# A four-layer network on one NeuronCore: VectorE's work, DRAM round trips and TensorE forms rearranged in layer 0 and layer 3

## The chip, the core and the metric

The kernel runs on one core of one Trainium2 chip. The metric is the device time of one execution in microseconds (us). The profile is one execution taken by the hardware profiler. PE is TensorE (its matmuls; an fp32 matmul is recorded as two passes), PEld its weight load, DVE is VectorE, ACT is ScalarE, POOL is GpSimd, SP is SyncE, whose queue issues most DMAs. Lines (L271) are lines of the kernel before.

## The reference, cut to what matters

The input x has the shape [2, 96, 48, 48]. Four layers follow one another, each of the form x + layer(groupnorm(x)). Layer 0 is a selective scan in four directions with E = 192 channels, N = 16 states and L = 2304 positions:

```python
xz = einsum('bchw,oc->bohw', x, in_proj_w)
xi, z = split(xz, 2, axis=1)
xi = silu(conv2d(xi, conv_w, conv_b, groups=E, pad=1))     # 3x3 depthwise
xs = stack([xf, xf[..., ::-1], xt, xt[..., ::-1]], axis=1)  # four directions
dlt, b, c = ...                                             # projections of xs
dlt = softplus(dt_proj(dlt) + dt_proj_b)
dA = dlt[..., None] * A_log
phi = exp(-cumsum(dA))
h = phi * cumsum(dlt * b * xs / (phi + 1e-12))
y = einsum('bkdln,bknl->bkdl', h, c) + Ds
ys = y1 + y2 + y3 + y4      # each turned back into image order
yn = layernorm over channels(ys) * ln_g + ln_b
u = yn * z                  # then 1x1, depthwise 3x3, 1x1, SE gate
```

Layer 1 forms sums of products of channel pairs, layer 2 is a 9x9 depthwise convolution. Layer 3 splits the channels in three: a gated 3x3 convolution (conv0), a fractional Fourier transform with a gated channel mix and its inverse, and a real FFT with the same; the three parts, concatenated, go through a 3x3 convolution with 96 channels (conv2), whose result is added to x. Both spectral mixes add a constant per channel: `Mix = group_conv(Mix, conv05_w * Y) + conv05_b`.

## The kernel before, in words

Every stage is a function with a block of its own: each engine has its instruction list, engines meet at semaphores, and at the end of a block all of them meet. The order within an engine is the order of the code. `ps` is all of PSUM, eight banks of 512 fp32 columns. The E x batch = 384 rows of layer 0 lie in T = 3 tiles of 128 partitions.

- **l0_project** (L182 to L284). TensorE makes xi and then z in chunks of 384 columns, 18 each; ScalarE copies them out of PSUM, xi into a padded image `pad`, z into `Z`. Each tile has nine depthwise taps of 2304 columns, 27 in all: ScalarE forms eight as products (L250), three of them as a tile's first term and five that GpSimd adds (L284), and VectorE does the other 19 as multiply-adds (L271). Then Silu (L254).
- **l0_steps** (L287 to L592). The step sizes softplus(x), made from e = exp(-|x|) and ln(1 + e) with a correction for the rounding of 1 + e, in 36 units of 768 columns. Per unit TensorE projects into a PSUM slot (L431; two slots for the first eight units, three afterwards), ScalarE does Abs, Ln of the unit before, Exp (L485, L490, L493), VectorE does four operations (`rounded` L521, L527, L532, and L537 that makes `dl` and frees the slot), GpSimd forms v = dl * xs (L585), and SP stores dl and v to DRAM. GpSimd and SP also do the weight products of layer 1 here, `wa*ma + wb*mb` in cuts of 8 (L565, L567, L570), with loads and stores between those of dl and v.
- **l0_scan** (L595 to L868). 36 units of 16 steps of 768 columns. In each step ScalarE forms decay and tanh, VectorE scans (L800) and multiplies (L774, L781), GpSimd multiplies (L811, L820), and TensorE broadcasts rows of b and c (L704) and sums the 16 products in PSUM with an identity (L737). After a unit ScalarE copies the sum out (L832) and its queue stores it to DRAM `y`, 36 stores of 384 KB.
- **l0_norm** (L871 to L1005). The twelve `y` arrays are loaded again and nine VectorE additions turn and add them (L971, L973), then the layernorm: mean by TensorE (L924), centring (L980), squares, variance (L930), reciprocal (L988), root, spread to the rows (L939), and the product with Z (L1004).
- **l3_gates** (L1510 to L1653). Gates on small matmuls; SP stores the normalised input, loads it turned (`xh`, L1551) and spreads three shifted copies of 32 channels into `G0` row by row (L1558).
- **l3_forward** (L1656 to L1827). Transform over rows (L1722 and L1728), over columns (L1736 for the fractional one, L1746 for the FFT, two products each, summed in PSUM), the channel mix in five chunks `fr` (L1756) with a one-row matmul that adds the constant (L1758), VectorE's phases as tables of 2304 columns (L1803, L1804), and a mix for the FFT (L1763). Results go to DRAM.
- **l3_inverse** (L1830 to L2024). conv0 for both images (L1935, 36 matmuls), four inverse transforms (L1944, L1952, L1959, L1968), results `P` and `F` stored to DRAM (L1904, L1909) and loaded back turned into `cat` (`to_cat`, L1898), all by SP, each store waited for before its load is issued; then conv2 (L1977) and the final addition into X (L2023). A last block stores X.

## Time and profile before

| | us |
|---|---|
| median of 3 runs | 3286.42 (3284.29 to 3290.19) |
| the profiled execution | 3293.45 |
| its span, first to last instruction | 3291.6 |
| l0_project | 25.7 to 113.9 |
| l0_steps | 114.4 to 346.9 |
| l0_scan | 350.9 to 2075.2 |
| l0_norm | 2078.0 to 2191.6 |
| l3_gates (after its group norm) | 3003.1 to 3021.3, next stage from 3032.4 |
| l3_forward | 3032.4 to 3126.5 |
| l3_inverse | 3130.8 to 3283.0 |
| output | to 3291.6 |

The start and end of a stage are the first and last record of its lines. Because engines meet at every stage's end, each stage can be read for itself: which engine's work ended it, and what that engine waited for. An engine that is busy for most of the span (VectorE 81%) is not the bound in every stage.

### The profile page before, as it was taken

How to read it: one execution, taken by the hardware profiler on the slowest of the kernel's cores; microseconds unless marked ns; L12 is line 12 of the kernel's file. 1: busy time of each engine (PE TensorE's matmuls, PEld its weight loads, DVE VectorE, ACT ScalarE, POOL GpSimd, SP SyncE). 2: the span in 40 equal slices, each digit the busy share in tenths (PEclk: the TensorE clock that was granted, in tenths of full speed). 3: DMA queues.
4: the chain of work that ended last, by engine and by line, in shares of the span. 5: the costliest groups of instructions: out<-in, count | busy, mean ns of one | idle time of the engine just before them, and what ended most of it. 6: DMA issues, size and time to landing. Idle time of an engine off the chain costs nothing. (4 is left out here: it accounts for less than half of the span.)

```text
span 3291.6 us, 24792 instructions
## 1 busy us (share of the span) xinstructions
PE 2159.3 (66%) x7226; PEld 1034.3 (31%) x7226; DVE 2659.7 (81%) x2092; ACT 1607.6 (49%) x2295; POOL 2126.9 (65%) x1113
## 2 busy tenths in 40 slices
PE   3454366666666666666666666488409897893958
PEld 1221123222332323323232333232105453452634
DVE  7677699999999999999999999668846566896200
ACT  4454477677767766777677677135300000641120
POOL 4166699999999999999999999107230000791000
PEclk8776699999999999999999999766759898896679
DMA  1176443344344333443444343500058885004050
GB/s 43 50 206 224 148 127 117 115 124 127 110 128 127 123 110 122 128 125 112 124 127 121 111 125 112 202 0 0 0 160 316 274 311 173 22 8 62 15 65 22
DMA packets 161258, 388.16 MB, mean 118 GB/s; under 512 B 60577, under 2 KB 70441, under 8 KB 147945
## 3 DMA queue, kind: packets, MB, share of 16 engines
q1 hardware_dynamic: 155400, 368.37, 36.8%
q10 hardware_dynamic: 5730, 18.29, 1.6%
q8 instruction: 56, 0.92, 0.1%
q14 instruction: 72, 0.59, 0.1%
...
## 5 line engine op out<-in xcount | busy, mean ns | idle before, releaser
L811 POOL TENSOR_TENSOR l0c_r<-l0c_r,l0c_v 128x768 f32<-128x768 f32 x576 | 1040.1, 1821 | 23.9 <-DVE l0c_r L774 22.8
L839 ACT ACTIVATE ps<-l0c_dlt,l0c_na 128x512 f32<-128x512 f32 (+1 forms) x1152 | 626.0, 575 | 517.0 <-DVE l0c_h L800 492.7
L820 POOL TENSOR_TENSOR l0c_hcp<-l0c_cb,l0c_h 128x768 f32<-128x768 f32 x384 | 698.7, 1820 | 0.7 <-DVE l0c_h L800 0.6
L800 DVE TENSOR_TENSOR_SCAN l0c_h<-ps,l0c_h,l0c_r 128x768 f32<-128x768 f32 x384 | 693.2, 1805 | 5.0 <-issue 5.0
L864 ACT ACTIVATE l0c_r<-l0c_S,l0c_floor,l0c_na 128x768 f32<-128x768 f32 x576 | 583.5, 1014 | 14.2 <-ACT l0c_y L832 14.2
L737 PE MATMUL ps<-l0c_hcp,net_ident 128*128 128x512 f32 (+1 forms) x1536 | 582.3, 502 | 9.0 <-ACT l0c_y L832 6.0
L704 PE MATMUL ps<-l0c_Bp,l0c_sel 96*128 96x512 bf16 (+1 forms) x1152 | 294.1, 338 | 439.9 <-DVE l0c_hcv L781 258.2
L774 DVE SCALAR_TENSOR_TENSOR l0c_r<-l0c_r,ps 128x768 f32<-128x768 f32 x576 | 533.1, 925 | 6.8 <-PE ps L704 4.1
L737 PEld LDWEIGHTS ps<-l0c_hcp,net_ident 128*128 128x128 f32 x1536 | 269.7, 196 | 256.1 <-issue 199.4
L1297 PE MATMUL ps<-l_prod,l_wa 128*96 128x384 f32 (+1 forms) x888 | 291.3, 492 | 86.9 <-DVE l_prod L1281 86.9
L800 DVE TENSOR_TENSOR_SCAN l0c_h<-ps,l0c_r 128x768 f32<-128x768 f32 x192 | 334.9, 1744 | 0.0
L1281 DVE TENSOR_TENSOR l_prod<-l_base,l_other 128x2304 f32<-128x2304 f32 (+1 forms) x74 | 189.3, 2558 | 138.7 <-PE ps L1297 88.2
L737 PE MATMUL ps<-l0c_hcv,net_ident 128*128 128x512 f32 (+1 forms) x768 | 289.8, 500 | 1.1
L704 PEld LDWEIGHTS ps<-l0c_Bp,l0c_sel 96*128 96x128 bf16 x1152 | 86.0, 98 | 618.7 <-DVE l0c_r L774 526.7
...
L1297 PEld LDWEIGHTS ps<-l_prod,l_wa 128*96 128x96 f32 (+1 forms) x888 | 146.3, 165 | 231.3 <-issue 143.7
L1187 POOL TENSOR_TENSOR l_Z<-l_Z,l0f_prod 128x2304 f32<-128x2304 f32 x13 | 85.1, 6557 | 184.7 <-ACT l0f_prod L1108 184.1
...
L704 PE MATMUL ps<-l0c_Cp,l0c_sel 96*128 96x256 bf16 (+1 forms) x384 | 96.4, 333 | 158.9 <-DVE l0c_r L774 157.6
L781 DVE TENSOR_TENSOR l0c_hcv<-ps,l0c_h 128x768 f32<-128x768 f32 x192 | 181.9, 947 | 0.0
L1493 PE MATMUL ps<-l_rows,l_diag 128*128 128x384 f32 x450 | 154.7, 506 | 33.6 <-ACT l_diag L1399 19.3
L737 PEld LDWEIGHTS ps<-l0c_hcv,net_ident 128*128 128x128 f32 x768 | 134.6, 195 | 124.8 <-issue 99.1
...
## 6 DMA issues: line engine op xcount, KB each, us to landing
l0c_cb<-cf SPq DMA_DIRECT2D x768, 192.0 KB, 3.4
l_other<-po SPq DMA_DIRECT2D x72, 1152.0 KB, 5.1
...
l0n_yk<-y SPq DMA_DIRECT2D x9, 1152.0 KB, 8.4
```

The lines of the kernel that those rows point to most:

```text
L704: mm = pe.matmul(ps[:, lo:hi], sel[:, t % 2, n * 128:(n + 1) * 128], rows[:, i, lo - at:hi - at], start=True, stop=True)
L737: mm = pe.matmul(ps[:, lo:hi], ident[:, :], hc[:, lo - PY:hi - PY], start=(n == 0), stop=(n == N - 1))
L774: dve.scalar_tensor_tensor(rj, rj, 1.0, b_all, ALU.add, ALU.mult).then_inc(s_ub, 1)
L781: dve.tensor_tensor(hcv[:, dve_steps(j) % NHV, :], c_all, h[:, j % N, :], ALU.mult).then_inc(s_hv, 1)
L800: dve.tensor_tensor_scan(h[:, n, :], da[j % 2], r[:, j % NR, :], init, ALU.mult, ALU.add).then_inc(s_scan, 1)
L811: pool.tensor_tensor(r[:, j % NR, :], r[:, j % NR, :], v[:, (j // N) % 2, :], ALU.mult).then_inc(s_w, 1)
L820: pool.tensor_tensor(hcp[:, p % NHP, :], cb[:, p % NCB, :], h[:, e % N, :], ALU.mult).then_inc(s_hp, 1)
L839: act.activation(da[e % 2][:, part], dlt[:, i, part], ACT.Exp, scale=na[:, i, n:n + 1]).then_inc(done, 1)
L864: act.activation(r[:, j % NR, :], S[:, i, :], ACT.Tanh, bias=floor[:, :], scale=na[:, i, N + n:N + n + 1]).then_inc(s_tanh, 1)
L1281: dve.tensor_tensor(prod[0:n, s, :], base[0:n, s, :], other[0:n, s, :], ALU.mult).then_inc(s_prod, 1)
L1297: mm = pe.matmul(ps[0:C, c * BANK:c * BANK + CH], wa[0:height[i], i, :], prod[0:height[i], i % 3, c * CH:(c + 1) * CH], start=(i == 0), st ...
L1493: mm = pe.matmul(ps[:, o:o + CH], diag[:, tl, i, :], rows[:, tl, dy + 8 * c:dy + 8 * c + 8, dx:dx + W], start=(i == 0), stop=(i == NPE - 1))
```

## The change

It touches layer 0 up to its norm and layer 3; layers 1 and 2 and the ffn are as they were.

- **load, l0_project**: the projection's weights are loaded with x. Only the edges of `pad` are zeroed. xi's 18 chunks are copied out by ScalarE and VectorE in turn. Taps 0 to 2 become matmuls with diagonal matrices (made by GpSimd) into PSUM banks 0 to 5, VectorE does the six others on halves of a tile (1152 columns, 36 in all), the first of them reading PSUM. z's chunks lie between, through banks 6 and 7. GpSimd's additions and ScalarE's products are gone.
- **l0_steps**: u = 1 + e is made by ScalarE (Identity with a bias), then Ln(u); VectorE's L521 is gone and its next operation forms (u - 1) - ln. Four buffers of dl and v instead of three. v is stored one unit later than dl. The layer-1 weight products are no longer here. Z is stored to DRAM at the start (3.5 MB).
- **l0_scan**: the sum of a unit stays in SBUF, in `Y`, which takes Z's place, in image order. For the second to fourth direction TensorE adds what Y holds to the unit's sum with identity matmuls in steps 4 to 7 (27 units of 36), and ScalarE writes the whole back, the last direction with the scale and the sum of Ds. ScalarE's tanh runs one step late for five steps after that.
- **l0_norm**: no y loads, no additions. Z is loaded again. The layer-1 weight products are made here by GpSimd, in cuts of 5, with their loads and stores.
- **l3_gates**: G0's three copies are spread as whole contiguous rows of 2304 elements and the wrong edge columns zeroed afterwards.
- **l3_forward**: row transforms write two groups of partitions (0 and 64), so that the two column products become one matmul with twice the contraction: 192 passes of L1736 become 96, 384 of L1746 become 192. The one-row matmuls are gone; their term is a table `u1` that VectorE forms once and adds.
- **l3_inverse**: conv0 of the second image comes after the inverse transforms. P and F are stored by ScalarE's queue, each on a semaphore of its own; SP only loads. X is stored in 12 parts as conv2's chunks end.

Cut to its core, the diff is:

```diff
+                if j >= 2:
+                    pe.wait_ge(s_tap, OWN * (j - 2) + 1)
+                for i in range(MM):
+                    dy, dx = divmod(i, 3)
+                    for c in range(HB):
+                        y0 = 8 * (HB * half + c) + dy
+                        mm = pe.matmul(ps[:, bank(HB * (j % 2) + c)], diag[:, t, i, :],
+                                       pad[:, t, y0:y0 + 8, dx:dx + W], start=(i == 0), stop=(i == MM - 1))
+                mm.then_inc(s_sum, 1)
...
+                for n, i in enumerate(range(MM, TAPS)):
                     dy, dx = divmod(i, 3)
                     if n:
-                        dve.wait_ge(s_tap, sum(own[:t]) + n)
-                    dve.scalar_tensor_tensor(dst, pad[:, t, dy:dy + H, dx:dx + W], cw[:, t, i:i + 1], dst,
-                                             ALU.mult, ALU.add).then_inc(s_tap, 1)
+                        dve.wait_ge(s_tap, OWN * j + n)
+                    dve.scalar_tensor_tensor(
+                        dst, pad[:, t, r0 + dy:r0 + dy + 8 * HB, dx:dx + W].rearrange("p (c h) w -> p c h w", h=8),
+                        cw[:, t, i:i + 1], dst if n else total, ALU.mult, ALU.add).then_inc(s_tap, 1)
...
                     act.wait_ge(s_e, i)
-                    if i >= 2:
-                        act.wait_ge(s_a, i - 1)
-                    act.activation(ps[:, LN:LN + SEG], e[:, (i - 1) % NE, :], ACT.Ln, bias=1.0).then_inc(s_ln, 1)
+                    if i > NW:
+                        act.wait_ge(s_q, i - NW)
+                    act.activation(u[:, (i - 1) % NW, :], e[:, (i - 1) % NE, :], ACT.Identity, bias=one_col[:, :]
+                                   ).then_inc(s_u, 1)
                 if i < U:
                     act.wait_ge(s_ab, i + 1)
                     act.activation(e[:, i % NE, :], e[:, i % NE, :], ACT.Exp, scale=-1.0).then_inc(s_e, 1)
+                if i:
+                    act.wait_ge(s_u, i)
+                    if i >= 2:
+                        act.wait_ge(s_a, i - 1)
+                    act.activation(ps[:, LN:LN + SEG], u[:, (i - 1) % NW, :], ACT.Ln).then_inc(s_ln, 1)
...
-            def rounded(i):
-                dve.wait_ge(s_e, i + 1)
-                dve.tensor_scalar(wm[:, i % NW, :], e[:, i % NE, :], 1.0, -1.0, ALU.add, ALU.add).then_inc(s_wm, 1)
-
-            rounded(0)
             for i in range(U):
                 dve.wait_ge(s_ln, i + 1)
-                dve.wait_ge(s_wm, i + 1)
-                dve.tensor_tensor(ln, wm[:, i % NW, :], ln, ALU.subtract).then_inc(s_q, 1)
-                if i + 1 < U:
-                    rounded(i + 1)
+                dve.scalar_tensor_tensor(ln, u[:, i % NW, :], 1.0, ln, ALU.subtract, ALU.subtract).then_inc(s_q, 1)
...
+        def so_far(u):
+
+            t, k, c0 = place(u)
+            return scan_order(Y[:, t, :], k)[:, c0 // W:(c0 + SEG) // W, :]
+
+        def y_pieces(u):
+
+            k, full = place(u)[1], BANK // W
+            if k < 2:
+                flat = Y[:, place(u)[0], ::-1] if k else Y[:, place(u)[0], :]
+                c0 = place(u)[2]
+                return [(PY, PY + BANK, flat[:, c0:c0 + BANK]), (PY + BANK, PY + SEG, flat[:, c0 + BANK:c0 + SEG])]
+            rows, cut = so_far(u), BANK % W
+            return [(PY, PY + full * W, rows[:, 0:full, :]),
+                    (PY + full * W, PY + BANK, rows[:, full, 0:cut]),
+                    (PY + BANK, PY + BANK + W - cut, rows[:, full, cut:W]),
+                    (PY + BANK + W - cut, PY + SEG, rows[:, full + 1:SEG // W, :])]
...
+                if place(u)[1] and 4 <= n < 4 + len(y_pieces(u)):
+                    lo, hi, src = y_pieces(u)[n - 4]
+                    pe.matmul(ps[:, lo:hi], ident[:, :], src, start=False, stop=False)
...
+                src = y_all.rearrange("p (r c) -> p r c", c=W)
+                if k < K - 1:
+                    act.activation(so_far(u), src, ACT.Copy).then_inc(s_evac, 1)
+                else:
+                    act.wait_ge(s_dsum, 1)
+                    act.activation(so_far(u), src, ACT.Identity, scale=0.5, bias=dsum[:, t:t + 1]).then_inc(s_evac, 1)
...
+                late = 0 < u < U and LAG + 3 <= n < LAG + 8
+                if j < J and not late:
+                    if 0 < u and n == LAG + 8:
+                        tanh(j - 1)
+                    tanh(j)
+                elif late and n > LAG + 3:
+                    tanh(j - 1)
...
+                lo, hi = max(0, 1 - i), L - max(0, i - 1)
                 for b in range(B):
-                    sp.dma_start(G0[C3 * i:C3 * i + C3, b, 1:1 + H, lo + 1 - i:hi + 1 - i],
-                                 by_image(XG[0:C3, b, :])[:, :, lo:hi]).then_inc(s_spread, 16)
+                    sp.dma_start(G0[C3 * i:C3 * i + C3, b, :, :].rearrange("c h w -> c (h w)")[:, W + lo:W + hi],
+                                 XG[0:C3, b, lo + i - 1:hi + i - 1]).then_inc(s_spread, 16)
...
-                        for s in range(2):
-                            mm = pe.matmul(ps[BC * q:BC * q + BC, o:o + UH],
-                                           A2[:, :, :, s, u].rearrange("p b c -> p (b c)"),
-                                           fw[:, s, UH * q:UH * q + UH], start=(s == 0), stop=(s == 1))
+                        mm = pe.matmul(ps[BC * q:BC * q + BC, o:o + UH], A2[:, :, :, u].rearrange("p b c -> p (b c)"),
+                                       fw[:, UH * q:UH * q + UH], start=True, stop=True)
                 mm.then_inc(s_mm, 1)
-            pe.wait_ge(s_in, 32)
+            pe.wait_ge(s_ed, evac_count(q_c1 - 1))
             for i, (lo, hi) in enumerate(FCH):
                 n = (hi - lo) * H
-                pe.wait_ge(s_ed, evac_count(q_c0 + i))
-                for w, b, q in ((wg[:, 0, :, :, :], bw, q_fr + 2 * i), (ws[:, :, :, :], bws, q_fr + 2 * i + 1)):
+                for w, q in ((wg[:, 0, :, :, :], q_fr + 2 * i), (ws[:, :, :, :], q_fr + 2 * i + 1)):
                     free(q)
                     pe.matmul(ps[:, bank(q, n)], w.rearrange("p q b o -> p (q b o)"),
-                              Z[:, lo:hi, :].rearrange("p j k -> p (j k)"), start=True, stop=False)
-                    pe.matmul(ps[:, bank(q, n)], b[:, :, :].rearrange("p q n -> p (q n)"), e11[:, lo * H:hi * H],
-                              start=False, stop=True).then_inc(s_mm, 1)
+                              Z[:, lo:hi, :].rearrange("p j k -> p (j k)"), start=True, stop=True).then_inc(s_mm, 1)
...
+            step(dve.tensor_scalar(u1[:, :, :], PA[:, :, :], bwc[:, 0:1], None, ALU.mult))
+            step(dve.scalar_tensor_tensor(u1[:, :, :], PB[:, :, :], bwc[:, 1:2], u1[:, :, :], ALU.mult, ALU.add))
+            step(dve.tensor_tensor(u1[:, :, :], u1[:, :, :], e11[:, :, :], ALU.mult))
...
-                sp.wait_ge(s_root, g + 1)
-                sp.dma_start(d["o"][0, :, lo:hi, :], P2[:, lo:hi, :]).then_inc(s_pst, 16)
-                sp.wait_ge(s_pst, 16 * (g + 1))
+                sp.wait_ge(s_pst[g], 16)
                 to_cat(0, lo, hi)
             for i, (lo, hi) in enumerate(K2):
-                sp.wait_ge(s_ea, evac_count(q_2 + i))
-                sp.dma_start(d["o"][1, :, 2 * lo:2 * hi, :], F[:, 2 * lo:2 * hi, :]).then_inc(s_fst, 16)
-                sp.wait_ge(s_fst, 16 * (i + 1))
+                sp.wait_ge(s_fst[i], 16)
                 to_cat(1, 2 * lo, 2 * hi)
...
+                act.wait_ge(s_root, g + 1)
+                act.dma_start(d["o"][0, :, lo:hi, :], P2[:, lo:hi, :]).then_inc(s_pst[g], 16)
             for i, (lo, hi) in enumerate(K2):
                 act.wait_ge(s_mm, q_2 + i + 1)
                 act.copy(F[:, 2 * lo:2 * hi, :].rearrange("p c w -> p (c w)"), ps[0:D2, bank(q_2 + i, (hi - lo) * 2 * W)]
                          ).then_inc(s_ea, 1)
+                act.wait_ge(s_ea, evac_count(q_2 + i))
+                act.dma_start(d["o"][1, :, 2 * lo:2 * hi, :], F[:, 2 * lo:2 * hi, :]).then_inc(s_fst[i], 16)
+            conv0(1)
```

On TensorE in l0_project, before, the 48 chunk matmuls stand in one piece (`XG` is the normalised input, `w_in` the weights):

```order
5 L222 MATMUL ps<-l0x_XG,l0p_w_in 128x384 x6
6 L222 MATMUL ps<-l0x_XG,l0p_w_in 64x384 x12
7 L222 MATMUL ps<-l0x_XG,l0p_w_in 128x384 x12
8 L222 MATMUL ps<-l0x_XG,l0p_w_in 64x384 x12
9 L222 MATMUL ps<-l0x_XG,l0p_w_in 128x384 x6
```

And with the change, where `pad` and `diag` are the padded xi and the diagonal taps:

```order
5 L220 MATMUL ps<-l0x_XG,l0w_w_in 128x384 x6
6 L220 MATMUL ps<-l0x_XG,l0w_w_in 64x384 x12
7 L220 MATMUL ps<-l0x_XG,l0w_w_in 128x384 x6
8 L240 MATMUL ps<-l0p_pad,l0p_diag 128x384 x9
9 L220 MATMUL ps<-l0x_XG,l0w_w_in 128x384 x3
10 L240 MATMUL ps<-l0p_pad,l0p_diag 128x384 x9
```

The xi chunks come first as before; then each half tile has nine tap matmuls and three chunks of z behind them.

On ScalarE at the start of l0_steps' loop, before (e and ln of a unit, `na` a small table, `bc` a copy of b and c):

```order
20 L485 ACTIVATE l0s_e<-ps 128x768
21 L493 ACTIVATE l0s_e<-l0s_e 128x768
22 L495 ACTIVATE l0s_na<-l0e_A 128x12x16
23 L496 ACTIVATE l0s_na<-l0e_A 128x12x16
24 L485 ACTIVATE l0s_e<-ps 128x768
25 L490 ACTIVATE ps<-l0s_e 128x768
26 L493 ACTIVATE l0s_e<-l0s_e 128x768
27 L461 COPY l0s_bc<-ps 64x384 x4
```

And with the change (`u` is the new 1 + e):

```order
23 L472 ACTIVATE l0s_e<-ps 128x768
24 L481 ACTIVATE l0s_e<-l0s_e 128x768
25 L488 ACTIVATE l0s_na<-l0e_A 128x12x16
26 L489 ACTIVATE l0s_na<-l0e_A 128x12x16
27 L472 ACTIVATE l0s_e<-ps 128x768
28 L477 ACTIVATE l0s_u<-l0s_e,l0s_one_col 128x768
29 L481 ACTIVATE l0s_e<-l0s_e 128x768
30 L486 ACTIVATE ps<-l0s_u 128x768
31 L448 COPY l0s_bc<-ps 64x384 x4
```

Ln has moved from before Exp to behind it, and 1 + e is a fourth operation of each unit.

On TensorE in l3_inverse, before:

```order
2928 L1935 MATMUL ps<-l_G,l_w0g 32x384 x36
2929 L1944 MATMUL ps<-l3i_ei,l3i_Vj 96x96 x32
2930 L1952 MATMUL ps<-l3i_ei,l3i_A 96x96 x32
2931 L1959 MATMUL ps<-l3i_ih,l3i_Mu 100x192 x16
2932 L1968 MATMUL ps<-l3i_iw,l3i_A 96x96 x32
2933 L1977 MATMUL ps<-l3i_cat,l3i_w 96x384 x108
```

And with the change:

```order
3018 L1968 MATMUL ps<-l_G,l_w0g 32x384 x18
3019 L1979 MATMUL ps<-l3i_ei,l3i_Vj 96x96 x32
3020 L1987 MATMUL ps<-l3i_ei,l3i_A 96x96 x32
3021 L1994 MATMUL ps<-l3i_ih,l3i_Mu 100x192 x16
3022 L2003 MATMUL ps<-l3i_iw,l3i_A 96x96 x32
3023 L1968 MATMUL ps<-l_G,l_w0g 32x384 x18
3024 L2014 MATMUL ps<-l3i_cat,l3i_w 96x384 x108
```

Half of conv0 has moved behind the last inverse transform, ahead of conv2.

## Rows read from the trace of the kernel before

**Rows 1.** The page: the granted TensorE clock in 40 slices, in tenths.

```profile
PEclk8776699999999999999999999766759898896679
```

**Rows 2.** Groups by line in l0_project: busy us, mean ns, idle before.

```profile
L271 DVE SCALAR_TENSOR_TENSOR l0p_acc<-l0p_pad,l0p_cw,l0p_acc 128x2304 f32<-128x2304 f32 x19 | 72.9, 3846 | 5.7 <-ACT l0p_acc L250 5.1
L284 POOL TENSOR_TENSOR l0p_acc<-l0p_acc,l0p_prod 128x2304 f32<-128x2304 f32 x5 | 35.2, 7051 | 44.6 <-ACT l0p_prod L250 44.4
L222 PE MATMUL ps<-l0x_XG,l0p_w_in 96*128 96x384 f32 (+1 forms) x96 | 31.3, 592 | 25.8 <-ACT l_Z L238 15.1 <-DMA l0p_cb<-in_cb 8.1 <-ACT l0p_pad L240 2.5
```

**Rows 3.** Windows of L271 (us, busy, clock, DMA share, GB/s); a group of l2_diffuse.

```profile
53.49:82.70 29.21, 29.11 (x5) 0.64 0.00 1
85.28:98.50 13.22, 13.08 (x6) 0.50 0.00 0
...
L1473 DVE SCALAR_TENSOR_TENSOR ps<-l_rows,l_kern,ps 128x1152 f32<-128x1152 f32 x108 | 153.7, 1423 | 3.8
```

**Rows 4.** Groups by line in l0_steps, 114 to 350 us.

```profile
L431 PE MATMUL ps<-l0s_P,l0e_w_up 128*128 128x512 f32 (+1 forms) x144 | 83.7, 726 | 91.5 <-DVE l0s_dl L537 91.5
L521 DVE TENSOR_SCALAR l0s_wm<-l0s_e 128x768 f32<-128x768 f32 x36 | 47.6, 1321 | 5.1 <-ACT l0s_e L493 5.1
...
L537 DVE SCALAR_TENSOR_TENSOR l0s_dl<-ps,l0s_e 128x768 f32<-128x768 f32 x36 | 34.5, 957 | 26.2 <-DMA dlt<-l0s_dl 23.4 <-DVE l0s_e L532 0.9 <-POOL l0s_vv L585 0.9
```

**Rows 5.** VectorE's timeline (start, length, idle before), then one window (PE, PEld, DVE, ACT, POOL).

```profile
316.27 0.96 DVE L537 SCALAR_TENSOR_TENSOR l0s_dl<-ps,l0s_e 128x768 f32<-128x768 f32 x1 [8.86 <-DMA dlt<-l0s_dl]
...
206.50:214.95 8.45, 5.85 (x8) 2.34 (x8) 7.69 (x8) 6.50 (x8) 3.63 (x2) 0.50 1.01 171
```

**Rows 6.** The scan, 400 to 2070 us: engines' busy times in one window, and one group.

```profile
400.00:2070.00 1670.00, 1110.98 (x3765) 505.47 (x3766) 1663.63 (x1351) 1172.96 (x1724) 1666.01 (x941) 0.97 0.40 120
...
L737 PE MATMUL ps<-l0c_hcp,net_ident 128*128 128x512 f32 x1512 | 573.5, 503 | 8.9 <-ACT l0c_y L832 6.0 <-POOL l0c_hcp L820 2.9
```

**Rows 7.** Groups in l0_norm, then one piece of TensorE's timeline.

```profile
L924 PE MATMUL ps<-l_Y,l0n_avg 128*128 128x384 f32 x84 | 30.8, 531 | 38.3 <-DVE l_Y L973 38.3
L973 DVE TENSOR_TENSOR l_Y<-l0n_yk,l_Y 128x2304 f32<-128x2304 f32 x6 | 24.3, 4055 | 1.7 <-DMA l0n_yk<-y 1.4
...
L971 DVE SCALAR_TENSOR_TENSOR l_Y<-l0n_yk,l0n_dsum,l_Y 128x2304 f32<-128x2304 f32 x3 | 7.9, 2619 | 8.5 <-DMA l0n_yk<-y 8.5
...
2146.25 13.46 PE L930 MATMUL ps<-l0n_sq,l0n_avgv 128*2 128x384 f32 x36 [2.80 <-ACT l0n_sq L946]
```

**Rows 8.** SyncE's timeline and a group of DMAs in l3_gates.

```profile
3015.46 10.82 SPq L1558 DMA_DIRECT2D l_G<-l3x_XG  x6
...
g<-l3x_XG SPq DMA_DIRECT2D x1, 1152.0 KB, 4.5
```

**Rows 9.** TensorE's timeline in l3_forward, then one VectorE group.

```profile
3050.86 10.87 PE L1736 MATMUL ps<-l3w_ef,l3w_A 128*64 128x48 f32 x190
3061.52 23.57 PE L1746 MATMUL ps<-l3w_fw,l3w_A 128*64 128x25 f32 x384
3085.02 1.97 PE L1756 MATMUL ps<-l3f_Z,l3w_wg 128*128 128x480 f32 x2
3086.92 1.96 PE L1758 MATMUL ps<-l3f_e,l3w_bw 1*128 1x480 f32 x2
...
L1804 DVE TENSOR_TENSOR l3f_u<-l3w_cs 128x2304 f32<-128x2304 f32 x2 | 5.1, 2558 | 0.1
```

**Rows 10.** l3_inverse: TensorE's and ScalarE's timelines, then DMA shares and one issue.

```profile
3130.87 26.47 PE L1935 MATMUL ps<-l_G,l_w0g 96*32 96x384 f32 x72 [4.83 <-PEq L1661]
...
3209.39 72.98 PE L1977 MATMUL ps<-l3i_cat,l3i_w 96*96 96x384 f32 x216 [30.36 <-DMA l3i_cat<-o]
...
3145.76 0.57 ACT L1988 ACTIVATE l3i_cat<-ps,l3i_b 32x384 f32<-32x384 f32 x1 [1.36 <-PE ps L1935]
...
q1 hardware_dynamic: 6944, 2.36, 52.8%
...
out<-net_X SPq DMA_DIRECT2D x1, 1728.0 KB, 7.9
```

522 lines of the change are left out of this document (259 added, 263 removed).

## The prediction

> **What bounds the kernel now.** I first read the busy time and the granted clock by slices [rows 1]: the middle two thirds is the scan at nearly full clock, and the dips to half clock lie at both ends, where the change works. Every stage ends with all engines meeting, so I take each one by its own limit and add up. All times of the sum are of the profiled execution (3293.45 us, span 3291.6), which lies 7 us above the median, 3286.42; I carry the difference over to the median.
>
> In l0_project VectorE's taps are the limit, and they are slow for a reason: the groups show a mean of 3846 ns and GpSimd's additions at 7051 ns [rows 2]. Between 53.49 and 82.70 us four taps take 29.1 us, 7.3 each, beside GpSimd; between 85.28 and 98.50, with GpSimd idle, five take 2.6 each (the window counts one more at its edge) [rows 3]. In l0_steps nobody is busy all the time; the loop through TensorE, ScalarE and VectorE is the limit, plus waits for stores [rows 4, 5]. In the scan VectorE and GpSimd are both busy for over 99.5% of 1670 us, TensorE for 1111 [rows 6]. In l0_norm TensorE waits 38 us for the additions [rows 7]. l3_forward is TensorE alone [rows 9], l3_inverse TensorE, then a 30 us wait for a chain of stores and loads, then conv2 [rows 10].
>
> **l0_project: -16 us.** Removed are the whole-image memsets, the five GpSimd additions and 19 long taps. VectorE now has 36 taps of 1152 columns. A multiply-add of that size reading PSUM took 1423 ns in l2_diffuse with GpSimd busy beside it [rows 3]; half of 2.6 is 1.3. I take 1.45 with issue: 52 us. They can begin after the 18 chunk copies; the first matmul stood at 28 us and 36 passes of 0.3 to 0.6 us [rows 2] end by some 40 to 45 us. So the end is 43 + 52 + 2 for the last Silu, 98 instead of 113.9. Nine tap matmuls and three chunks per half are 24 to 30 passes: at 0.32 us 8 to 10 us, as long as VectorE's 8.7, so hidden by a hair; at half clock 16 us, and the stage would be 13 us longer than before. The clock in the old stage is 0.64 and 0.50 because TensorE had finished [rows 3]; now it never stops. Range -18 to -8, with +13 as the far end.
>
> The slow taps are what the Trainium skill states ("SBUF — State Buffer", who interferes with whom): a VectorE instruction with two SBUF inputs contends with a GpSimd one that reads SBUF, one with an input in PSUM does not. The trace agrees, 7.3 against 2.6 and 1.42 unharmed. By it five of six new taps could still be hit, but only by the nine small diagonal products, so the sum is the same.
>
> **l0_steps: -20 us.** Removed: L521, 1321 ns in the mean (47.6 us in all), and the layer-1 products, with their transfers. Added: one ScalarE operation per unit and a 3.5 MB store at the start. In the undisturbed window 206.50 to 214.95 two units take 8.45 us at half clock, TensorE 2.93 per unit [rows 5]. A loop spans two units: TensorE's product, then Abs and Ln (0.81 each, eight operations of ScalarE in 6.50 us [rows 5]), VectorE's three (0.96 with overlap 0.9) and L521 beside GpSimd: 2.9 + 1.6 + 2.7 + 1.15 = 8.4, as seen. With the change Identity and Exp stand in the path between Abs and Ln and L521 is out: 2.9 + 3.3 + 2.7 = 8.9 at half clock, 7.5 at full. So the clean loop gains nothing, or 0.5 us a unit: 3.75 to 4.5 a unit, I take 4.4. The gain is in the waits: VectorE idles 26.2 us ahead of L537, 23.4 of it for stores of dl still under way, one of 8.86 us [rows 4, 5]. Fewer transfers, four buffers and a store of v that no longer holds up dl's should end nearly all of it. 26 us less, and 6 that I leave standing for waits that the new store of Z and the slower start bring: -20. Range -10 (half of the waits stay, since Z's store and DMAs of b and c still stand there) to -36 (full clock).
>
> **l0_scan: 0 us, up to +15.** VectorE and GpSimd set the step of 2.98 us, and neither gets work. TensorE gets one identity matmul in 4 steps of 27 units, up to 0.5 us x 2 passes in a step in which it is idle for a third (1111 of 1670 [rows 6]). ScalarE loses nothing, its store is as long (0.8) and its late tanh eats from six buffers. What no row prices is TensorE reading Y at a stride of 192 bytes in 18 units. The nearest rows: VectorE's turned addition took 4055 ns against 2619 for the straight one [rows 7], a factor 1.55. With it 2 x 0.5 becomes 1.6 us, against idle 1.0 us per step: late by 0.6 in two steps of 18 units, 20 us at worst if no buffer took it, and there are four. I take +0.5. Range -3 to +15.
>
> On strides the Trainium skill ("SBUF — State Buffer", the DMA port swizzle) says that each access which crosses to a new 16-byte line pays; VectorE's 1.55 agrees, and for TensorE no row here shows it. By that rule at a factor of 2 the scan would be 10 to 20 us longer; that is the rival below.
>
> **l0_norm: -31.5 us.** The mean matmuls waited 38.3 us for VectorE's additions [rows 7] and L930 began at 2146.25. Now only the 448 KB table `avg` stands ahead: 84 passes, 30.8 us, from 2080.5, then squares 2.1: L930 at 2113. That is 33; GpSimd's products beside VectorE's centring give back 1.5. The layer-1 products' chain (3.5 MB of Z and 10 MB of loads and stores, at g's pace of 256 GB/s [rows 8] 53 us, with 24 operations beside them) ends near 2140 to 2150, and VectorE's end is at 2160: covered. If each cut takes 9 us instead of 5 it ends last, at 2178, costing 18. Range -35 to -15.
>
> **l3_gates: -7.** The spread's issue alone took 10.82 us [rows 8] in rows of 192 bytes; 1.7 MB in long rows, at the pace of `g` (1152 KB in 4.5 us [rows 8]), is 6.6. The next stage starts at 3025.5 instead of 3032.4. Range -9 to -5.
>
> **l3_forward: -38.** L1736 goes from 192 passes in 11.2 us to 96 of twice the columns (between half of it and all of it: 8.5), L1746 from 23.57 to half, 11.8. The fr stage is 36.6 us of matmuls, every second one with one row [rows 9]: ten are left, 18.3 at the same half clock, 9.2 at full, 12.7 if it recovers as conv2's did after 6 us. In all 94 - 2.4 - 11.8 - 24 = 56. VectorE ends at about the same time: three phases 23, waiting for columns, the table 6.6 (three operations of up to 2.56 [rows 9]), then 5 x 2.6: also 55. So -38; -32 at half clock throughout, -39 where VectorE is last. The page's 7 tenths there says half clock in part.
>
> **l3_inverse: -25.5.** conv0's 36 matmuls took 26.47, the sixth chunk was out at 3145.76. The 13 us behind it (11.6 for the half that moves) now stand where TensorE waited 30.36 us [rows 10]. DMAs start 11.6 to 13 earlier and no longer one after another; but the queues were already in use for 52.8% of the 39 us from 3171 [rows 10]. Packed tight, that is 20.6 us, and a last load of 5: conv2 starts 54 us into the stage instead of 78.5. TensorE bound, it would be 48.5. Its first chunk ran at half clock, about 1.2 us of that goes. Range -32 to -20. **Output**: 12 stores behind the chunks instead of one of 7.9 us [rows 10], the last one some 2: -5.3.
>
> **Sum.** +0.3 (weights with x) - 16 - 20 + 0.5 - 31.5 - 7 - 38 - 25.5 - 5.3 = -142.5. 3286.4 - 142.5 = **3144 us**.
>
> **Rivals.** (a) Full clock where I take half: l0_steps -36, l3_forward and inverse a few more. -165, 3121 us. For it: TensorE is given denser work in both. Against: 0.50 in the window of rows 5 with TensorE busy 5.85 of 8.45. (b) The strided re-addition or the late tanh stalls the scan, or the layer-1 products end l0_norm last: 15 to 20 of the gain lost, 3162. For: no row for TensorE's strided read. Against: GpSimd and VectorE have buffers of four and six. (c) The stages' gains don't appear since work was only moved: in l0_project TensorE at half clock becomes the limit (+13 instead of -16), and l3_forward's table ends last: 3175. For: the margin in l0_project is a hair. (d) Slower: the clock in the scan. TensorE's work per step is 1111/1670 x 2.98 = 2.0 us at clock 0.97 [rows 6]; at half clock it is 3.9, 0.9 more than the step, 530 us for 576 steps. If the re-additions and their waits brought half clock for over 27% of the scan, all 142 would be gone; at half the scan 3410 us. Against it: the work gets denser, not thinner, and clock stood at 0.97.
>
> **How the numbers follow.** Forecast (3130 to 3158) 0.55; (a) 0.15; (b) 0.17; (c) 0.08; (d) 0.03; the rest lies between. The range takes the forecast, most of (a) and (b): 3115 to 3172. A measurement of this kernel tells 0.2%, 6.6 us. Faster: all but (d) and a little, 0.96; same 0.01; slower 0.03.
>
> **What would show it.** In the profile after: L284's taps at 1.3 to 1.45 us; no idle time of VectorE for dl's stores; the scan at 2.98 us per step with TensorE's idle smaller; TensorE in l0_norm with no wait for VectorE ahead of the means, and the root reached by 2130; 96 and 192 passes in l3_forward and VectorE and TensorE ending within 3 us; conv2 starting 54 us into l3_inverse with the wait ahead of it about 6 us. Wrong would be: GpSimd last in l0_norm, TensorE last in l0_project, a clock below 0.9 in the scan.

## The result, and the profile after

The changed kernel takes **3149.35 us** (median of 4 runs, 3146.08 to 3150.87) against 3288.31 of the kernel before (median of 4, 3284.29 to 3293.59). The ratio is 0.9575, with a 95% interval of 0.9559 to 0.9592: 139 us faster. Forecast were 3144 us, with a range of 3115 to 3172. The profiled executions, 3293.45 before and 3148.91 after, differ by 144.5 us, and it is between these two that the stages are compared (in the table each change is after minus before, us; where a row runs to the next stage, the pause at the stage's end is in it):

| | forecast | before | after | change |
|---|---|---|---|---|
| start to l0_project | +0.3 | 25.7 | 25.6 | -0.1 |
| l0_project, to the next stage | -16 | 88.6 | 75.7 | -12.9 |
| l0_steps, to the next stage | -20 | 236.5 | 215.9 | -20.6 |
| l0_scan, first to last record | +0.5 | 1724.3 | 1731.1 | +6.8 |
| l0_norm, from the scan's last record | -31.5 | 117.0 | 80.7 | -36.3 |
| untouched stages between | 0 | 811.0 | 810.2 | -0.8 |
| l3_gates, to the next stage | -7 | 29.2 | 25.9 | -3.3 |
| l3_forward, to the next stage | -38 | 98.5 | 50.2 | -48.3 |
| l3_inverse | -25.5 | 152.2 | 129.3 | -22.9 |
| output | -5.3 | 8.6 | 2.4 | -6.2 |

The page of after, busy time per engine and the granted TensorE clock in 40 slices, to be laid beside [rows 1]:

```profile
PE 2207.9 (70%) x7334; PEld 1072.0 (34%) x7334; DVE 2572.6 (82%) x2080; ACT 1624.5 (52%) x2316; POOL 2092.8 (67%) x1126
...
PEclk9876799999999999999999999986666989799689
```

In the whole span VectorE lost 87 us of work and TensorE gained 49. The mean granted clock rose from 0.871 to 0.890.

**l0_project.** VectorE's timeline (start, length, operation, idle time before in brackets) shows its first tap; the groups of the stage (busy us, mean ns, idle) follow:

```profile
47.86 1.41 DVE L284 SCALAR_TENSOR_TENSOR l0p_acc<-l0p_pad,l0w_cw,ps 128x1152 f32<-128x1152 f32 x1 [6.26 <-PE ps L240]
```

```profile
L284 DVE SCALAR_TENSOR_TENSOR l0p_acc<-l0p_pad,l0w_cw,l0p_acc 128x1152 f32<-128x1152 f32 x30 | 42.6, 1419 | 1.1
L240 PE MATMUL ps<-l0p_pad,l0p_diag 128*128 128x384 f32 x108 | 36.1, 488 | 0.7 <-issue 0.7
```

The taps take 1419 ns each, and the six that read PSUM 1410, where the old ones took 3846 in the mean [rows 2, 3]. But the first tap begins at 47.9, not at 43: the nine tap matmuls of the first half tile (6.0 us) come behind the last chunk, and VectorE waits for them, 6.26 us. Later ones are hidden.

**l0_steps.** The groups of l0_steps in the profile of after, against [rows 4]:

```profile
L417 PE MATMUL ps<-l0s_P,l0e_w_up 128*128 128x512 f32 (+1 forms) x144 | 84.2, 728 | 77.5 <-DVE l0s_dl L523 77.1
...
L515 DVE SCALAR_TENSOR_TENSOR ps<-l0s_u,ps 128x768 f32<-128x768 f32 x36 | 34.7, 963 | 88.2 <-ACT ps L486 87.9
L523 DVE SCALAR_TENSOR_TENSOR l0s_dl<-ps,l0s_e 128x768 f32<-128x768 f32 x36 | 34.5, 957 | 1.2
...
L477 ACT ACTIVATE l0s_u<-l0s_e,l0s_one_col 128x768 f32<-128x768 f32 x36 | 33.3, 926 | 0.0
```

No wait for a store of dl is left ahead of L523, where 23.4 us stood ahead of L537. Instead VectorE waits 87.9 us for ScalarE's Ln at L515, before 35.6 at L527. From unit 8 to 22 dl comes mostly every 2.99 and 6.08 us in turn (once after 11.85), and later in other pairs of about the same sum: 9.07 for two units where the undisturbed loop before took 8.45 [rows 5].

**l0_scan.** The groups of the scan in the profile of after:

```profile
L770 DVE SCALAR_TENSOR_TENSOR l0c_r<-l0c_r,ps 128x768 f32<-128x768 f32 x576 | 533.8, 927 | 14.5 <-PE ps L695 9.4 <-issue 2.6 <-ACT l0c_r L847 2.4
...
L733 PE MATMUL ps<-l_Z,net_ident 128*128 128x480 f32 (+5 forms) x180 | 74.9, 502 | 0.0
...
L830 ACT ACTIVATE l_Z<-ps 128x768 f32<-128x768 f32 x27 | 27.4, 1016 | 0.0
...
L833 ACT ACTIVATE l_Z<-ps,l0c_dsum 128x768 f32<-128x768 f32 x9 | 14.0, 1550 | 5.4 <-PE ps L728 5.4
```

VectorE idles 14.5 us ahead of L770; its twin of before, L774, had 6.8 on the page. ScalarE's write back to Y takes 788 ns where rows are contiguous. At a stride of 192 bytes it takes 1.46 to 1.48 us as a copy and 1.54 to 1.56 with the scale and the sum of Ds (27 writes of 1016 ns in the mean, 18 of them contiguous, and nine of 1550).

**l0_norm.** TensorE's timeline there: the mean matmuls begin 4.2 us after the stage's first DMA issue, and in one piece; L947, the twin of L930 of [rows 7], 36.0 us after that issue, before 68.3:

```profile
2053.00 28.89 PE L940 MATMUL ps<-l_Z,l0n_avg 128*128 128x384 f32 x84 [6.26 <-DMA l0n_avg<-in_avg]
2084.79 11.77 PE L947 MATMUL ps<-l0n_sq,l0n_avgv 128*2 128x384 f32 x36 [2.89 <-ACT l0n_sq L963]
```

**l3_gates.** The spread's issue by SyncE, then GpSimd's first edge memset behind it:

```profile
2951.53 7.61 SPq L1571 DMA_DIRECT2D l_G<-l3x_XG  x6
```

```profile
2964.11 0.25 POOL L1585 MEMSET l_G<- 32x96 f32 x1 [20.59 <-DMA l_G<-l3x_XG]
```

**l3_forward.** TensorE's timeline, to be laid beside [rows 9], and three rows of VectorE's, the end of its table, its first product and its last:

```profile
2965.17 5.36 PE L1740 MATMUL ps<-l3w_ef,l3w_xh 96*48 96x48 f32 x128 [12.74 <-PEq L1527]
2970.30 5.76 PE L1748 MATMUL ps<-l3w_fh,l3w_xh 96*48 96x96 f32 x128
2975.87 6.26 PE L1757 MATMUL ps<-l3w_ef,l3w_A 128*64 128x96 f32 x96
2981.95 10.87 PE L1766 MATMUL ps<-l3w_fw,l3w_A 128*64 128x25 f32 x192
2992.74 1.97 PE L1774 MATMUL ps<-l3f_Z,l3w_wg 128*128 128x480 f32 x2
```

```profile
2996.55 2.56 DVE L1841 TENSOR_TENSOR l3f_u<-l3f_u,l3f_e 128x2304 f32<-128x2304 f32 x1
2999.14 0.66 DVE L1849 TENSOR_TENSOR l3f_v<-ps,l3f_PA 128x480 f32<-128x480 f32 x1
...
3010.86 0.56 DVE L1853 TENSOR_TENSOR l3f_V<-l3f_v,l3f_u 128x384 f32<-128x384 f32 x1
```

TensorE's last matmul ends at 3005.5 and VectorE at 3011.4: VectorE is last, after 46 us with hardly a pause.

**l3_inverse.** TensorE's timeline, and what share the two DMA queues had of 3044 to 3070 us:

```profile
3015.36 15.11 PE L1968 MATMUL ps<-l_G,l_w0g 96*32 96x384 f32 x36 [9.86 <-PEq L1673]
...
3046.56 5.60 PE L2003 MATMUL ps<-l3i_iw,l3i_A 100*96 100x96 f32 x64
3052.09 11.80 PE L1968 MATMUL ps<-l_G,l_w0g 96*32 96x384 f32 x36
3071.40 72.51 PE L2014 MATMUL ps<-l3i_cat,l3i_w 96*96 96x384 f32 x216 [7.51 <-issue]
```

```profile
q1 hardware_dynamic: 6272, 1.18, 65.4%
q10 hardware_dynamic: 672, 1.18, 20.2%
```

conv2 begins 56.1 us into the stage (before 78.5), with a wait of 7.5 us in place of 30.36 [rows 10]. In 26 us the two queues fill 85.6% where one filled 52.8% of 39.

### The profile page after: what moved, and what is told of

It reads as the page before. It is cut to its first block and busy times, and to the rows that moved or that the text cites. A ratio compares the mean times of both kernels' runs of the same rounds, so it can differ in the third digit from the quotient of the medians.

```text
span 3147.0 us, 24979 instructions
## 1 busy us (share of the span) xinstructions
PE 2207.9 (70%) x7334; PEld 1072.0 (34%) x7334; DVE 2572.6 (82%) x2080; ACT 1624.5 (52%) x2316; POOL 2092.8 (67%) x1126
## 5 line engine op out<-in xcount | busy, mean ns | idle before, releaser
L728 PE MATMUL ps<-l0c_hcp,net_ident 128*128 128x512 f32 (+1 forms) x1536 | 597.5, 514 | 14.1 <-ACT l_Z L830 7.3
L770 DVE SCALAR_TENSOR_TENSOR l0c_r<-l0c_r,ps 128x768 f32<-128x768 f32 x576 | 533.8, 927 | 14.5 <-PE ps L695 9.4
L1400 POOL TENSOR_TENSOR l_accp<-l_accp,l_prod 128x1152 f32<-128x1152 f32 x54 | 142.3, 2637 | 29.9 <-ACT l_prod L1425 22.3
```

The lines of the kernel that those rows point to most:

```text
L728: mm = pe.matmul(ps[:, lo:hi], ident[:, :], hc[:, lo - PY:hi - PY], start=(n == 0), stop=(n == N - 1))
L770: dve.scalar_tensor_tensor(rj, rj, 1.0, b_all, ALU.add, ALU.mult).then_inc(s_ub, 1)
```

## The experiments

Each one changes the changed kernel unless it says the kernel before. Times of a stage in them come from one profiled execution. In profiles of the same code the scan was 1728.2 to 1732.7 us long (eight of them), l0_steps 211.5 to 214.3 (six) and l3_inverse 126.1 to 131.4 (nine), so 2 or 3 us say nothing in the first two, and 5 us say nothing in l3_inverse. In those nine conv2 started 52.9 to 57.4 us into its stage.

### The scan without the re-additions

```diff
-                if place(u)[1] and 4 <= n < 4 + len(y_pieces(u)):
-                    lo, hi, src = y_pieces(u)[n - 4]
-                    pe.matmul(ps[:, lo:hi], ident[:, :], src, start=False, stop=False)
```

> The changed kernel without the identity matmuls that add Y to a unit's sum in l0_scan, so the four directions are not added up. With the change the scan takes 1731.1 us against 1724.3 before; VectorE idles about 0.5 us at the 14th step of ten of the 18 units of the turned directions, each time after a slice of half clock. Theory A (the re-added pieces, the 240-column one above all, make TensorE late when it meets half clock): the scan is 5 us shorter, 1726, and the idle times at step 14 are gone, the two of 1.4 us at step 7 stay. Theory B (ScalarE's late tanh and its store with rows of 192 bytes, 1.5 us instead of 0.8, are the cause): the scan stays at 1730 to 1731 and the idle times stay where they are.

Measured: 3139.1 us, the scan 1725.5 instead of 1731.1. The group that idled 14.5 us idles 8.4:

```profile
L767 DVE SCALAR_TENSOR_TENSOR l0c_r<-l0c_r,ps 128x768 f32<-128x768 f32 x576 | 533.3, 926 | 8.4 <-PE ps L695 5.7 <-ACT l0c_r L844 2.4
```

All idle times at the step named are gone. In place of the two of 1.4 us in the middle of a unit there are two of 0.8 us, in other units. ScalarE's strided write and its late tanh are still in this kernel, and its scan is only 1.2 us above the 1724.3 before, so no cost of theirs shows beyond the spread. Theory A holds: the re-additions cost some 5 us (5.6 between these two profiles, 2.7 to 7.2 against all eight). The trace of the change gives the same sum by another way: VectorE idles 0.39 to 0.67 us at that step in eleven of the 18 turned units, 5.7 us in all. How the re-additions do it is to be seen in one unit of the turned direction after the change:

```profile
694.80 1.79 DVE L760 TENSOR_TENSOR_SCAN l0c_S<-l0c_dlt,l0c_S,ps 128x768 f32<-128x768 f32 x1
...
697.49 0.73 PE L695 MATMUL ps<-l0c_Bp,l0c_sel 96*128 96x512 bf16 x2 [2.28 <-DVE l0c_r L770]
...
698.01 2.77 PE L728 MATMUL ps<-l0c_hcp,net_ident 128*128 128x512 f32 x4
...
700.57 0.99 PE L733 MATMUL ps<-l_Z,net_ident 128*128 128x240 f32 x2
...
701.73 0.49 PE L695 MATMUL ps<-l0c_Bp,l0c_sel 96*128 96x512 bf16 x2
...
702.31 0.95 DVE L770 SCALAR_TENSOR_TENSOR l0c_r<-l0c_r,ps 128x768 f32<-128x768 f32 x1 [0.58 <-PE ps L695]
```

VectorE makes a cumulative sum (L760), TensorE has nothing to do for 2.28 us, and its granted clock is 0.5 from 697.6 to 701.0. The four passes that follow take 2.77 us where they take 1.46 at full clock. Behind them stands the piece of 240 columns, and only then the rows of b for VectorE, which waits 0.58 us. In the four turned units without half clock there (the one that starts at 1181 us, say) VectorE doesn't wait. In three others it doesn't wait although the half clock falls there, so the two together aren't always enough. In the nine units of the second direction it never waits; their pieces are read in contiguous rows, but they are also only two, and none stands at that step. What a stride of 192 bytes costs TensorE is to be seen at full clock, the first piece of a turned unit, 480 columns, against that of a unit of the second direction, 512 columns:

```profile
641.48 1.77 PE L733 MATMUL ps<-l_Z,net_ident 128*128 128x480 f32 x2
```

```profile
546.57 1.02 PE L733 MATMUL ps<-l_Z,net_ident 128*128 128x512 f32 x2
```

1.77 us against 1.02. So it takes a piece of the re-addition and the half clock together. That the piece must be a strided one was not tried by itself.

### The re-additions at a later step

```diff
-                if place(u)[1] and 4 <= n < 4 + len(y_pieces(u)):
-                    lo, hi, src = y_pieces(u)[n - 4]
+                if place(u)[1] and 9 <= n < 9 + len(y_pieces(u)):
+                    lo, hi, src = y_pieces(u)[n - 9]
```

> The changed kernel with the re-additions of Y in steps 9 to 12 of a unit's sum instead of 4 to 7, away from VectorE's cumulative sums, behind which the clock falls for a slice. Theory A (piece and half clock meet): the idle times at step 14 go, scan 1726 to 1727, all 3144 to 3145 us. Theory B (any place costs the same, since TensorE has no room for the pieces, or the store is the cause): scan 1730 to 1731, idle times elsewhere.

Measured: 3147.55 us, the scan 1728.6. The idle times at the fourteenth step are gone as theory A has it, but others of 0.3 to 1.5 us came at a unit's start and in its middle. The length lies within what unchanged scans show. Inconclusive; the timed pair below settles it.

### 1 + e back on VectorE

```diff
-                    act.activation(u[:, (i - 1) % NW, :], e[:, (i - 1) % NE, :], ACT.Identity, bias=one_col[:, :]
-                                   ).then_inc(s_u, 1)
...
+                dve.tensor_scalar(u[:, i % NW, :], e[:, i % NE, :], 1.0, -1.0, ALU.add, ALU.add).then_inc(s_u, 1)
```

(Ln stands ahead of Exp again and reads e.)

> The changed kernel with l0_steps' 1 + e back on VectorE (the operation of before, Ln before Exp), all else of the change kept. Theory A (the loop of two units holds TensorE 2.9, two or four operations of ScalarE and VectorE's three; moving 1 + e to ScalarE made it longer, from 8.45 to 9.07 us, and the stage's gain is from the transfers alone): the stage is 6 to 10 us shorter than the 215.9 of the changed kernel, 206 to 210. Theory B (the removed 47.6 us of VectorE are what gave the 20 us): the stage goes back to 225 to 236.

Measured: 3143.65 us; the stage, to the next one, 206.9 us instead of 215.9. VectorE has its 46.9 us of L509 again and the stage is 9 us shorter:

```profile
L509 DVE TENSOR_SCALAR l0s_u<-l0s_e 128x768 f32<-128x768 f32 x36 | 46.9, 1303 | 5.1 <-ACT l0s_e L480 5.1
```

The period is mostly 4.17 to 4.22 us a unit. Theory A's forecast holds: 1 + e on ScalarE, with Ln behind Exp, cost 9 us, and what lies around it gained 29. What of that is due to the transfers of the layer-1 products that are gone, and what to storing v a unit later, was not tried apart.

But the loop that the theory names can account for the pace at half clock only. At full clock the period is 4.22 too, though TensorE's product takes 1.56 us there and not 2.93. This is one such period, VectorE's and ScalarE's rows, with the granted clock at 1.00:

```profile
289.96 0.81 ACT L477 ACTIVATE ps<-l0s_e 128x768 f32<-128x768 f32 x1 [0.86 <-DVE l0s_e L520]
...
290.80 0.96 DVE L515 TENSOR_TENSOR ps<-l0s_u,ps 128x768 f32<-128x768 f32 x1
...
291.68 1.54 DVE L509 TENSOR_SCALAR l0s_u<-l0s_e 128x768 f32<-128x768 f32 x1
...
293.14 0.94 DVE L520 SCALAR_TENSOR_TENSOR l0s_e<-ps,l0s_e 128x768 f32<-128x768 f32 x1
...
294.18 0.81 ACT L477 ACTIVATE ps<-l0s_e 128x768 f32<-128x768 f32 x1 [0.86 <-DVE l0s_e L520]
```

Ln (L477) has a single buffer in PSUM, and waits until VectorE has read the last one (L520), so a second loop, of four operations none of which is TensorE's, takes 4.22 us here.

### Ln first in ScalarE's order

```diff
             for i in range(U + 1):
+                if i:
+                    act.wait_ge(s_u, i)
+                    if i >= 2:
+                        act.wait_ge(s_a, i - 1)
+                    act.activation(ps[:, LN:LN + SEG], u[:, (i - 1) % NW, :], ACT.Ln).then_inc(s_ln, 1)
                 if i < U:
...
+                    act.activation(u[:, i % NW, :], e[:, i % NE, :], ACT.Identity, bias=one_col[:, :]
+                                   ).then_inc(s_u, 1)
```

(Abs and Exp stay between them, in that order.)

> The changed kernel with ScalarE's order in l0_steps changed to Ln of the unit before, Abs, Exp, 1 + e, so that no other unit's operation stands between a product's arrival and its own Ln. Theory A (the loop sets the pace; now it spans three units: 2.9 + 3.3 + 2.7 = 8.9 us for three, under ScalarE's own 3.4 us a unit): from unit 8 on 3.3 to 3.7 us a unit instead of 4.6, the stage 30 us shorter, 183 to 190 us, all about 3118. Theory B (TensorE's two products of 1.46 us at half clock, or the stores of 768 KB a unit, set the pace): 4.3 us or more a unit, the stage at most 8 us shorter.

Measured: 3118.49 us; the stage, to the next one, 184.1. The wait for Ln falls from 87.9 us to 54.7:

```profile
L513 DVE SCALAR_TENSOR_TENSOR ps<-l0s_u,ps 128x768 f32<-128x768 f32 x36 | 34.6, 961 | 54.7 <-ACT ps L472 54.7
```

From unit 21 on every period is 3.42 us. The granted clock was higher in this stage than with the change, and that is a rival for the gain; but six of the seven periods from unit 9 to 16 were 3.42 us as well, at a granted clock of 0.50, so the order is what counts. The 3.42 us are ScalarE's own work, as its timeline in a later run of the same kernel shows, four operations without a pause:

```profile
249.82 0.79 ACT L477 ACTIVATE l0s_e<-ps 128x768 f32<-128x768 f32 x1
250.64 0.84 ACT L479 ACTIVATE l0s_e<-l0s_e 128x768 f32<-128x768 f32 x1
251.52 0.94 ACT L483 ACTIVATE l0s_u<-l0s_e,l0s_one_col 128x768 f32<-128x768 f32 x1
252.49 0.82 ACT L472 ACTIVATE ps<-l0s_u 128x768 f32<-128x768 f32 x1
253.24 0.79 ACT L477 ACTIVATE l0s_e<-ps 128x768 f32<-128x768 f32 x1
```

Theory A holds. Ln ahead of Abs with 1 + e on VectorE was not tried.

### Three buffers of dl and v

```diff
-        NE, NW, ND = 3, 2, 4
+        NE, NW, ND = 3, 2, 3
```

> The changed kernel with three buffers of dl and v instead of four. Theory A (what ended the waits for stores is that the layer-1 products' transfers are gone and dl is stored ahead of v): the stage is the same within 3 us, and VectorE waits under 3 us for stores of dl. Theory B (the fourth buffer ended them): 10 us or more of such waits come back.

Measured: 3153.51 us; the stage 217.6 us from first to last record, 3 to 6 more than in the profiles with four buffers. VectorE's waits for dl stores come to 0.6 us in all. So the fourth buffer did not end them, theory A, though the stage is a little longer than A allows. 2.6 us of it are one longer period, 14.43 us instead of 11.85 behind the eleventh unit. In that period ScalarE waits for GpSimd's L532 ahead of its cast L465, 9.9 us where the change has 6.8; why GpSimd was later there wasn't followed up.

### Groups of partitions apart

```diff
-                for c in range(lo, hi):
-                    for g, r in enumerate(OFF):
+                for g, r in enumerate(OFF):
+                    for c in range(lo, hi):
```

(in both row transforms of l3_forward)

> The changed kernel with the row transforms' matmuls in another order: all of one group of 64 partitions in a chunk first, then all of the other, instead of in turn. With the change 128 passes of 96 columns took 5.6 us, before 64 of 192 took 10.4. Theory A (two matmuls that write to different halves of the partitions run beside each other, which is where the 48 us of l3_forward came from beyond the 38 forecast): the 128 passes of L1748 take 9 to 11 us, those of L1740 8 us at half clock, the stage up to 8 us longer where TensorE is last, less where VectorE is. Theory B (it is the smaller pass that is cheaper, whatever its neighbour writes to): 5.6 us again.

Measured: 3152.19 us, l3_forward 1.7 us longer (48.0 instead of 46.3), since VectorE then waits 1.4 us for columns (L1757).

```profile
2967.69 7.37 PE L1740 MATMUL ps<-l3w_ef,l3w_xh 96*48 96x48 f32 x125 [12.78 <-PEq L1527]
...
2975.06 6.83 PE L1748 MATMUL ps<-l3w_fh,l3w_xh 96*48 96x96 f32 x123
```

The 128 passes of L1740 take 7.5 us instead of 5.4, near A's 8; those of L1748 7.3 instead of 5.8, less than A's 9 to 11 (the rows above leave out a few passes at the ends). The starts of single passes at full clock explain L1748: where neighbours write to the same half of the partitions, a 96-column pass starts 83 ns after the one before; where they write to different halves, as with the change, two start 17 ns apart and the next pair 83 ns after the first of them; and around each change of group in this experiment some five passes start about 40 ns apart. So A's mechanism is there, and the new order only undoes part of it.

### The kernel before without the one-row matmuls

```diff
-                              Z[:, lo:hi, :].rearrange("p j k -> p (j k)"), start=True, stop=False)
-                    pe.matmul(ps[:, bank(q, n)], b[:, :, :].rearrange("p q n -> p (q n)"), e11[:, lo * H:hi * H],
-                              start=False, stop=True).then_inc(s_mm, 1)
+                              Z[:, lo:hi, :].rearrange("p j k -> p (j k)"), start=True, stop=True).then_inc(s_mm, 1)
```

> The kernel before with one part alone: the one-row matmuls that add the constant in l3_forward are left out, and so is the constant. Theory A (they cost as much as the full ones, and they keep the clock low, since it returned to full right after them): ten of twenty matmul pairs go, 18.3 us, and the rest runs at full clock after some 6 us: the stage is 22 to 26 us shorter, 72 to 76 us instead of 98.5 to the next stage. Theory B (the clock stays low whatever is in that stretch): 18 us shorter.

Measured: 3258.41 us, 29.5 under the kernel before, which took 3287.91 beside it. l3_forward is 65.5 us long instead of 94.1.

```profile
3082.89 1.97 PE L1756 MATMUL ps<-l3f_Z,l3w_wg 128*128 128x480 f32 x2
...
3087.68 0.97 PE L1756 MATMUL ps<-l3f_Z,l3w_ws 128*128 128x480 f32 x2
...
3092.99 2.18 PE L1761 MATMUL ps<-l3f_Fz,l3w_wg 128*128 128x500 f32 x6
```

The granted clock comes back to 1.00 4.6 us into the stretch, where it stayed at 0.50 to the end of the stage with the one-row matmuls. The ten matmuls take 10.1 us where twenty took 36.6, and the last mix 2.18 instead of 4.37. Theory A's mechanism holds; the 28.6 us are more than its 22 to 26, as the clock returned sooner than the 6 us I had taken from conv2.

### Both halves of conv0 in front

```diff
-        q_3 = NC
+        q_3 = B * NC
...
             conv0(0)
+            conv0(1)
             pe.wait_ge(s_V, 16 * 2 * B)
...
-            conv0(1)
             pe.wait_ge(s_ea, evac_count(q_c - 1))
```

> The changed kernel with both halves of conv0 ahead of the inverse transforms, as before; the stores stay on ScalarE's queue. With the change conv2 starts 56.1 us into l3_inverse, after 7.5 us of waiting for the loads. Theory A (the loads set the start of conv2, and they start behind conv0's second half): conv2 starts 11 to 12 us later, at 67 to 68. Theory B (the transfers then collide less with the loads of the stage's start and the wait shrinks): 60 to 63.

Measured: 3158.44 us. conv2 starts 67.1 us into the stage, 11.0 later than with the change, and the stage is 10.7 us longer. Theory A.

```profile
3081.28 8.93 PE L2014 MATMUL ps<-l3i_cat,l3i_w 96*96 96x384 f32 x20 [18.62 <-issue]
```

### P and F stored by SyncE

```diff
-                act.dma_start(d["o"][1, :, 2 * lo:2 * hi, :], F[:, 2 * lo:2 * hi, :]).then_inc(s_fst[i], 16)
...
+                sp.wait_ge(s_ea, evac_count(q_2 + i))
+                sp.dma_start(d["o"][1, :, 2 * lo:2 * hi, :], F[:, 2 * lo:2 * hi, :]).then_inc(s_fst[i], 16)
                 sp.wait_ge(s_fst[i], 16)
```

(and P in the same way)

> The changed kernel with P and F stored by SyncE's queue again, each waited for before its load is issued, and conv0 split as in the change. Theory A (the chain of six stores and loads takes 38 us from its start, which is now about 27 us into the stage): conv2 starts at 65 to 67 us instead of 56.1. Theory B (the transfers fill the queues anyway, so that who issues them is of no account): 56 to 58.

Measured: 3160.09 us. conv2 starts 64.9 us into the stage, 8.8 later than with the change. Theory A, at its lower edge.

```profile
3083.21 7.10 PE L2018 MATMUL ps<-l3i_cat,l3i_w 96*96 96x384 f32 x15 [17.63 <-issue]
```

The two parts of the change give 11 and 9 us of the 22.4 by which conv2 starts earlier. Within the spread of 4.5 us that the start of conv2 has from profile to profile they add up: neither hides the other.

### Both edits to the changed kernel, timed

Two kernels, each timed five times: Ln first alone, and Ln first with the re-additions at steps 9 to 12.

> The changed kernel with only ScalarE's order in l0_steps changed, timed in rounds beside the one with both edits: 3118 to 3120 us, a ratio of 0.948 to 0.949 to the kernel before.

> The changed kernel with both: Ln first in l0_steps' ScalarE order, and the re-additions in steps 9 to 12 of a unit's sum. If the later place of the re-additions is worth the 2 to 4 us that one look suggests: 3114 to 3117 us, and faster than the same kernel with only the ScalarE order changed. If it is worth nothing (the scan's length moves by 2 us from run to run with where the half-clock slices fall): both the same, 3118 to 3120.

Measured: Ln first alone 3117.33 us (3114.05 to 3119.84), ratio 0.9478, 95% interval 0.9465 to 0.9491; with both 3116.93 (3116.53 to 3121.93), ratio 0.9483, interval 0.9470 to 0.9496. No gain from the later place of the re-additions shows, and the intervals are too wide to rule out 2 us of it. Ln first by itself makes a kernel 32 us under the changed one.

## Why the prediction was right, point by point

The forecast of 3144 us was 5 off. That it is so near is luck in part: against the stages' sum the forecast missed 15.7 us in one direction (l0_project, l0_scan, l3_gates, l3_inverse) and 17.8 in the other (l3_forward and l0_norm above all), and these cancel. Three stages lie outside their own ranges: l3_forward (-32 to -39), l0_norm (-35 to -15) and l3_gates (-9 to -5). The shape of it holds: every stage that was to be shorter is, the scan's VectorE and GpSimd stayed the limit, l0_norm lost the wait of [rows 7], conv2's wait shrank, the scan's mean granted clock was 0.95 and not below 0.9 (rival d), and TensorE was not the limit in l0_project (rival c). By size:

- **l3_forward, -48.3 instead of -38.** The mechanism was right and the term mis-sized in two places. I took the row transforms as unchanged, 18.6 us; they took 11.1, because the two groups' matmuls overlap, 83 ns for two passes of 96 columns where one of 192 took 163. And I gave the ten matmuls at 12.7 us a clock that recovers after 6; it was back 2.1 us into them, and they took 9.0. The 96 passes of L1757 took 6.3 where I had 8.5. In the kernel before, the one-row matmuls alone were worth 28.6 us, as the experiment without them shows. With TensorE done after 40 us, VectorE ended the stage as said, but at 46 and not 55, since it hardly waited for columns; the two did not end within 3 us of each other but 5.9 apart.
- **l0_norm, -36.3 instead of -31.5.** L947 comes 32.2 us earlier in the stage, counted from its first DMA issue, against 33 forecast; the 1.5 us given back to GpSimd's products did not show (L982 takes 555 ns beside them, 551 before without), L947 itself took 11.8 us at full clock instead of 13.5, and the block's end no longer waits 2.8 us for the landing of the last y store, which I had not counted.
- **l0_scan, +6.8 instead of +0.5**, inside the +15 of the range, and rival (b) in part. The step of the argument that failed is "idle for a third" of a step: the mean hides the stretches of half clock behind VectorE's cumulative sums, in which TensorE has no third to spare. Some 5 us are the re-additions, as the run without them shows. The price I took for the stride from VectorE, 1.55, was too low: 1.59 us from the 480-column piece to the next matmul against 0.86 for 512 columns is a factor of 2 per column, and ScalarE's copy pays 1.9. The page "SBUF — State Buffer" of the Trainium skill, in its section on the DMA port swizzle, has each access that crosses to a new 16-byte line pay; both agree with it, and yet the scan lost 6.8 us and not 10 to 20, since at full clock the doubled piece still fits: none of the four turned units without half clock there has the wait.
- **l0_project, -12.9 instead of -16.** The taps cost 1.42 each as taken. What was left out is the filling of the pipeline, nine tap matmuls of 6.0 us ahead of the first tap. (The sum 43 + 52 + 2 gives 97, not the 98 written.)
- **l0_steps, -20.6 instead of -20.** The number is right, and its two terms have the right sign: the waits for stores are gone, and the loop did not gain. By size both are off and cancel: what lies around the loop gave 29.6 us (26 forecast, with 6 taken back for new waits), and the new order in ScalarE's list cost 9, where I had nothing. The formula gave 8.9 for two units at half clock, and 9.07 were measured. Its 7.5 at full clock, on which rival (a) rests, did not show: pairs with a unit at full clock in them took 8.4 to 9.1, and the run with 1 + e on VectorE shows the second loop, through Ln's one buffer, that the formula lacks.
- **l3_inverse, -22.9 instead of -25.5.** conv2 began at 56.1 and not 54, with the queues at 85.6% instead of packed tight. This miss of 2 us is within the spread of nine profiles of the same code, 52.9 to 57.4.
- **l3_gates, -3.3 instead of -7.** The pace of `g`, 256 GB/s, was no measure for the spread: from its first issue at 2951.5 to the memset at 2964.1 are 12.6 us for 1.7 MB beside what was left of the turned loads, 201 GB/s in the first eight and 137 after. Whether the 32 partitions of each spread or the queue's other transfers set it was not tried.
